# Building one-hot sets in two rings, with two weighted copies on POOL and the first normalisation inside the build

## The chip, the cores and the metric

The kernel runs as one program on one core of a Trainium2 chip. The metric is the device time of one execution in microseconds (us); lower is better. The core has five engines with instruction streams of their own: TensorE (PE), VectorE (DVE), ScalarE (ACT), GpSimd (POOL) and SyncE (SP), which here only issues DMAs. They meet through semaphores.

## The reference

Four graph layers run one after the other on 3125 nodes with 256 features, over 50000 edges sorted by their destination. Cut to what matters:

```python
h = relu(layernorm(x))                      # "the first normalisation"
x = x + sage(sage(h).relu())                # mean over incoming edges, twice
h = relu(layernorm(x))
x = x + segment_sum((h @ W)[src] * edge_weight[:, None], dst) + b
h = relu(layernorm(x))
x = x + interaction_layer(h, edge_attr, src, dst)   # sums over edges, layer norm, three-layer MLP
h = relu(layernorm(x))
x = x + h @ W_self + mean_over_edges(top32(h @ W_neigh)[src], dst)
```

Every layer needs sums over edges. The kernel gets them as products with two dense matrices of 3125 x 3125 (padded to 3200 x 3200): entry (s, d) of the count matrix is the number of edges from s to d, that of the weight matrix the sum of their weights.

## The kernel before

**The build.** The first third of the program makes the two matrices. There are 25 chunks (`NT`) of 128 destinations, and each has 8 tiles (`PER`) of 16 destinations (`G`), 200 tiles in all. The edges lie in edge tiles of 128, one edge per partition. For a tile the program walks over the edge tiles that touch it, three at a time (`RING = 3`; I call these three a group, and one edge tile of it a set). For one set, DVE writes two one-hot matrices: S (L877, 128 x 128: which of 128 residues the source has) and Q (L879, 128 x 400: destination and upper part of the source). The edge weight is split into three bf16 parts, W0, W1 and W2, so that their sum is exact; S times each part gives three weighted copies. Before, ACT makes the first two (L622, two instructions per set) and POOL the third (L579, one per set, after a small copy of the three weights, L576). PE then does four products per set: S with Q into the count bank, and the three copies with Q into the weight bank (L1271; its waits are, in this order, for Q, for ACT, for POOL). Where a tile is done, PE raises `s_built` with a tiny product (L1283), ACT copies the counts out of PSUM (`take`, L616) and DVE the weights (L871), both one tile late: the take of tile t-1 stands behind the work for tile t. After eight tiles SP stores the two blocks of the chunk to DRAM (L434, L438). The two PSUM banks of each matrix alternate from tile to tile.

**The ring.** There is one ring of three sets. DVE may write set u of a group when PE has used set u of the group before (`s_used`, wait in L875).

**The walk.** Each engine reads the bounds of its eight loops from a table at the start of a chunk (L350, eight values into registers) and steps through them on its own. PE and POOL loop over chunks; ACT and DVE have a loop whose body holds two chunks.

**Between build and first layer.** After the last tile DVE computes a scale for the first layer from the weights (L954 to L974, with two steps on PE, L1404 and L1408), waits for the last stores (the staging areas lie where the layer writes), and does the first normalisation for all 25 row blocks: statistics (L1000), one square root on ACT (L673), subtract and multiply (L1011), relu and scale (L1016). ACT makes the first f16 part (L679), POOL the second (L591). SP loads the late weights and then the first two count blocks, transposed (L495). Then PE starts the sums of the first layer (L1321), and within tile 1 the first transposes of its result (L1378).

## Time and profile before

| | |
|---|---|
| median of 3 runs | 1917.61 us (1917.14 to 1918.48) |
| the profiled execution | 1919.31 us |
| its span | 1917.4 us |
| PE busy | 1701.7 us, 89% |
| DVE busy | 1092.2 us, 57% |
| ACT busy | 759.1 us, 40% |
| POOL busy | 369.2 us, 19% |

The page of the profile cuts the span in 40 slices of 48 us:

```profile
PE   2999899999990999999997999999989898986996
DVE  5888788888888122222333666666536666665111
ACT  0988888989882111111111222222224333331000
POOL 1555555555553000000000000000011111110000
PEclk8999999999995999999998999999999999997998
```

A digit is the busy share of a slice in tenths, 9 for 90% or more; PEclk is TensorE's granted clock. Slices 2 to 12 are the build. There ACT and DVE stand at eight or nine tenths and POOL at five. In slice 13 PE has a zero: that is the stretch between build and first layer. All the rest of the program keeps PE at nine tenths nearly throughout.

### The profile page before, as it was taken

Reading aid. Unit: us, or ns where it says so; the run is one execution under the profiler, and the core shown is the slowest. Engines: PE = TensorE matmul, PEld = TensorE weight load, DVE = VectorE, ACT = ScalarE, POOL = GpSimd, SP = SyncE. Lnnn points to the kernel's source line nnn. Section 1 sums busy time; section 2 is a strip of 40 time slices with the busy share of each in tenths; the row PEclk is TensorE's granted clock in tenths of the full one; section 3 lists DMA queues with packets and bytes.
Section 4 is the critical chain, followed back from the end, with each engine's and each line's share of the span. In section 5 each row is a group of like instructions: output and inputs, shape, how many; then the busy total and the mean of one; then the engine's idle time right before and its main releaser. Section 6 shows DMA issues by size and latency. Waiting matters only on the chain.

```text
span 1917.4 us, 47392 instructions
## 1 busy us (share of the span) xinstructions
PE 1701.7 (89%) x11659; PEld 1292.2 (67%) x11660; DVE 1092.2 (57%) x3183; ACT 759.1 (40%) x2194; POOL 369.2 (19%) x982
## 2 busy tenths in 40 slices
PE   2999899999990999999997999999989898986996
PEld 1555555555550777777886888888867676764885
DVE  5888788888888122222333666666536666665111
ACT  0988888989882111111111222222224333331000
POOL 1555555555553000000000000000011111110000
PEclk8999999999995999999998999999999999997998
DMA  2544455445445556553334556565421212110444
GB/s 57 151 147 140 126 155 158 125 125 151 147 146 151 138 171 171 171 171 103 120 132 138 145 153 187 151 179 164 138 90 54 71 54 71 55 68 16 143 150 153
DMA packets 302401, 246.05 MB, mean 128 GB/s; under 512 B 144042, under 2 KB 286182, under 8 KB 302310
## 3 DMA queue, kind: packets, MB, share of 16 engines
q1 hardware_dynamic: 302310, 245.19, 43.0%
q14 instruction: 77, 0.63, 0.1%
q8 instruction: 14, 0.23, 0.0%
HBM read 138.17 MB, written 99.31 MB: 124 GB/s over the span
## 4 chain that ended last, share of the span: by engine, by line
issue 61%; PE 25%; DVE 5%; ACT 2%; POOL 2%; DVEq 1%; ACTq 1%; DMA 1%; SPq 0%; POOLq 0%
PE ps L1271 17%; PE ps L1321 7%; POOL work L601 2%; ACT front L622 2%; DVE front L879 1%; ACT work L616 1%; DVE front L877 1%; DMA wgt_blocks<-arena 0%; DVE work L1000 0%; PE ps L1256 0%; DVE arena L1011 0%; ACTq L350 0%; ACTq L359 0%; ACTq L622 0%; DVE arena L808 0%
## 5 line engine op out<-in xcount | busy, mean ns | idle before, releaser
L1321 PE MATMUL ps<-arena 128*128 128x256 f16 (+1 forms) x5000 | 607.1, 275 | 49.8 <-POOL arena L591 40.2
L1321 PEld LDWEIGHTS ps<-arena 128*128 128x128 f16 x5000 | 489.7, 98 | 147.2 <-issue 77.5
L1271 PE MATMUL ps<-front 128*128 128x400 bf16 x2580 | 482.9, 341 | 23.7 <-ACT front L622 20.0
L622 ACT ACTIVATE front<-front 128x128 bf16<-128x128 bf16 x1290 | 408.9, 391 | 57.6 <-issue 32.6
L1271 PEld LDWEIGHTS ps<-front 128*128 128x128 bf16 x2580 | 241.8, 99 | 196.2 <-ACT front L622 32.0
L1315 PE MATMUL ps<-arena 128*128 128x256 f32 x1250 | 281.3, 382 | 0.0
L579 POOL TENSOR_SCALAR front<-front,w_col 128x128 bf16<-128x128 bf16 x645 | 248.8, 392 | 163.0 <-DVE front L877 156.5
L601 POOL TENSOR_TENSOR work<-work 128x256 f32<-128x256 f32 x75 | 55.2, 736 | 1062.0 <-ACT work L742 1062.0
L1315 PEld LDWEIGHTS ps<-arena 128*128 128x128 f32 x1250 | 237.6, 192 | 31.8
L879 DVE TENSOR_SCALAR front<-iota,off_g,front 128x400 bf16<-128x400 f16 x645 | 253.5, 393 | 0.0
L877 DVE TENSOR_SCALAR front<-iota,front 128x128 bf16<-128x128 f16 x645 | 164.6, 255 | 91.0 <-PE ps L1271 70.0
L1456 PE MATMUL ps<-work,front 128*128 128x128 f32 x600 | 87.5, 292 | 38.7 <-POOL work L601 38.6
L871 DVE COPY arena<-ps 128x400 f32<-128x400 f32 x200 | 114.3, 572 | 1.0 <-PE ps L1283 1.0
L1456 PEld LDWEIGHTS ps<-work,front 128*128 128x128 f32 x600 | 77.9, 202 | 48.5 <-POOL work L601 45.9
L1025 DVE TENSOR_SCALAR rdeg<-ps 128x1 f32 (+1 forms) x25 | 4.0, 158 | 179.2 <-PE ps L1321 179.2
L646 ACT ACTIVATE work<-ps 128x256 f32<-128x256 f32 x75 | 28.8, 384 | 189.4 <-PE ps L1293 189.4
L616 ACT ACTIVATE work<-ps 128x400 f16<-128x400 f32 x200 | 96.8, 484 | 0.7 <-PE ps L1283 0.6
L641 ACT ACTIVATE small<-small 128x1 f32<-128x1 f32 x50 | 14.8, 295 | 186.3 <-DVE small L897 186.3
L1213 DVE SCALAR_TENSOR_TENSOR work<-ps,rdeg,arena 128x256 f32<-128x256 f32 x25 | 12.1, 484 | 112.9 <-PE ps L1321 112.9
L742 ACT ACTIVATE work<-ps,mlp_col 128x128 f32<-128x128 f32 x150 | 46.5, 361 | 66.2 <-PE ps L1456 66.1
L1051 DVE SCALAR_TENSOR_TENSOR work<-ps,rdeg_conv,arena 128x256 f32<-128x256 f32 x25 | 12.1, 484 | 93.8 <-PE ps L1321 93.8
L1097 DVE TENSOR_TENSOR e_hot<-iota,e_key 128x2304 bf16<-128x2304 f16 x25 | 64.0, 2559 | 1.9
(189 smaller groups left out, 1571.8 us busy)
## 6 DMA issues: line engine op xcount, KB each, us to landing
arena<-turned_blocks SPq DMA_DIRECT2D x75, 800.0 KB, 4.3
wgt_blocks<-arena SPq DMA_DIRECT2D x25, 1600.0 KB, 8.5
arena<-wgt_blocks SPq DMA_DIRECT2D x25, 1600.0 KB, 8.3
cnt_blocks<-work SPq DMA_DIRECT2D x25, 800.0 KB, 4.2
turned_blocks<-arena SPq DMA_DIRECT2D x25, 800.0 KB, 3.5
e_raw<-edge_features_padded SPq DMA_DIRECT2D x25, 576.0 KB, 7.9
edge_features_padded<-in_edge_attr SPq DMA_DIRECT2D x24, 512.0 KB, 9.6
out<-arena SPq DMA_DIRECT2D x24, 128.0 KB
```

Of the source, the lines that this page charges most:

```text
L579: pool.tensor_scalar(part_of(u, O_SW + 2 * P, P), part_of(u, O_S, P), w_col[:, u:u + 1], 1.0, ALU.mult, ALU.mult).then_inc(s_hotP, 1)
L601: pool.tensor_tensor(GT[l + 1], GT[l], YT, ALU.add).then_inc(s_g, 1)
L616: act.activation(stage_c[par][:, t, :], cnt_ps[t % 2][:, 0:GW], ACT.Copy).then_inc(s_taken, 1)
L622: m = act.activation(part_of(u, O_SW + a * P, P), part_of(u, O_S, P), ACT.Copy, scale=one(col[:, c, :], t))
L871: dve.tensor_copy(stage_w[par][:, t, :], wgt_ps[t % 2][:, 0:GW]).then_inc(s_takenW, 1)
L877: dve.tensor_scalar(part_of(u, O_S, P), iota1[:, 0:P], one(col[:, C_S, :], t), None, ALU.is_equal).then_inc(s_hotS, 1)
L879: dve.tensor_scalar(part_of(u, O_Q, GW), iota1[:, :], one(off_g, n), one(col[:, C_Q, :], t), ALU.add, ALU.is_equal).then_inc(s_hotQ, 1)
L1097: dve.tensor_tensor(e_hot[:, :, :], iota1[:, 0:P].rearrange("p (o d) -> p o d", o=1).broadcast_to([P, EC, P]), e_key[:, :].rearrange("p (t ...
L1271: return pe.matmul(out_, left, right, start=False, stop=True, skip_group_check=True)
L1315: m = pe.matmul(agg[par][:, 0:D], BLK32[par][:, b * P:(b + 1) * P], ZFULL[0][:, b * D:(b + 1) * D], start=(b == 0), stop=(b == NT - 1), sk ...
L1321: m = pe.matmul(agg[par][:, 0:wide], BLK16[par][:, b * P:(b + 1) * P], ZH[zin(i)][:, b * ZW + part * D:b * ZW + part * D + wide], start=(b ...
L1456: m = pe.matmul(mlp_ps[:, o * P:(o + 1) * P], W[:, k, o * P:(o + 1) * P], GT[l][:, k * P:(k + 1) * P], start=(k == 0), stop=(k == 1))
```

## The change

- There are two rings of three sets, and tile i of a chunk uses ring i % 2. The second lies in `e_part`, a tile that the third layer uses later. DVE keeps for each ring the number of sets after which it is free, and waits for that.
- POOL makes the copies for W1 and W2. It waits for all three S of a group and then issues two products of 128 x 3 x 128 elements, S by the weight broadcast along each set. The small copy of the weights and the drain before it go. PE waits for them apart, for W1 and for W2.
- ACT makes only the W0 copy, one instruction per set, and takes both matrices out of PSUM.
- The first normalisation of block c-1 is spread over chunk c on DVE, in five steps behind tiles 1, 2, 4, 5 and 6. The third step waits for a square root that ACT does behind tile 4. ACT makes the first part of block c-2 behind tile 2, POOL the second part behind tile 4. The multiplication by `H_SCALE` is folded into the square root.
- SP issues the two transposing loads of the first count blocks before the store of the last chunk.
- The scale of the first layer is computed at the start of that layer, on DVE in front of its first row step and on PE behind the sums of tile 0.

```diff
-        ring = front[:, 6 * NCOL:6 * NCOL + RING * SETW // 2].bitcast(BF16)
+        ring0 = front[:, 6 * NCOL:6 * NCOL + RING * SETW // 2].bitcast(BF16)
...
+        ring1 = e_part[:, :, :, :].rearrange("p t a f -> p (t a f)")[:, 0:RING * SETW]
+        ring = [r.rearrange("p (u s) -> p u s", u=RING) for r in (ring0, ring1)]
...
@@ SP
+            for n in range(2):
+                sp.wait_ge(s_store_c[n], 16)
+                sp.dma_start_transpose(BLK16[n].rearrange("p (b d) -> p b d", d=P),
+                                       cnt_dram[n * P:(n + 1) * P, :]).then_inc(s_blk[n], 16)
             store(NT - 1, 0)
...
@@ POOL
-                def weigh_last(k, u, t, i):
-                    if u == 0:
-                        pool.drain()
-                        chain(pool.tensor_copy(w_col[:, :], col[:, C_W2, bass.ds(t, RING)]))
-                    wait(pool, s_hotS, k + (u + 1))
-                    pool.tensor_scalar(part_of(u, O_SW + 2 * P, P), part_of(u, O_S, P), w_col[:, u:u + 1], 1.0,
-                                       ALU.mult, ALU.mult).then_inc(s_hotP, 1)
+                def weigh_sets(k, u, t, i):
+                    if u:
+                        return
+                    wait(pool, s_hotS, k + RING)
+                    plain = ring[i % 2][:, :, O_S:O_S + P]
+                    for a, col_of in ((1, C_W1), (2, C_W2)):
+                        into = ring[i % 2][:, :, O_SW + a * P:O_SW + (a + 1) * P]
+                        by = col[:, col_of, bass.ds(t, RING)].rearrange("p (t o) -> p t o", o=1)
+                        pool.tensor_tensor(into, plain, by.broadcast_to([P, RING, P]), ALU.mult
+                                           ).then_inc(s_hotP[a - 1], RING)
+                def after(t):
+                    if not isinstance(c, int) and t == 4:
+                        second(c - 2)
...
@@ ACT
             def take(c, par, t):
                 wait(act, s_built, c * PER + (t + 1))
                 act.activation(stage_c[par][:, t, :], cnt_ps[t % 2][:, 0:GW], ACT.Copy).then_inc(s_taken, 1)
+                act.activation(stage_w[par][:, t, :], wgt_ps[t % 2][:, 0:GW], ACT.Copy).then_inc(s_takenW, 1)
             def weigh(k, u, t, i):
                 wait(act, s_hotS, k + (u + 1))
-                for a, c in enumerate((C_W0, C_W1)):
-                    m = act.activation(part_of(u, O_SW + a * P, P), part_of(u, O_S, P), ACT.Copy,
-                                       scale=one(col[:, c, :], t))
-                m.then_inc(s_hotA, 1)
+                act.activation(part_of(i, u, O_SW, P), part_of(i, u, O_S, P), ACT.Copy, scale=one(col[:, C_W0, :], t)
+                               ).then_inc(s_hotA, 1)
+            def first_deviation(n):
+                wait(act, s_var0, n + 1)
+                act.activation(sd, mv[:, 1:2], ACT.Sqrt, bias=eps_first, scale=1.0 / H_SCALE ** 2).then_inc(s_std0, 1)
...
+                def after(t):
+                    late(t)
+                    if not (isinstance(c, int) and c == 0) and t == 4:
+                        first_deviation(c - 1)
+                    if not (isinstance(c, int) and c < 2) and t == 2:
+                        first_high(c - 2)
...
@@ DVE
+            def first_norm(n, step):
+                if step == 0:
+                    dve.bn_stats(bn, node(X, n))
+                elif step == 1:
+                    dve.drain()
+                    dve.bn_aggr(mv, bn).then_inc(s_var0, 1)
+                elif step == 2:
+                    wait(dve, s_std0, n + 1)
+                    dve.reciprocal(rs, sd)
+                elif step == 3:
+                    dve.drain()
+                    dve.tensor_scalar(node(R_, n), node(X, n), mv[:, 0:1], rs, ALU.subtract, ALU.mult)
+                else:
+                    dve.drain()
+                    dve.tensor_scalar(node(R_, n), node(R_, n), 0.0, None, ALU.max).then_inc(s_zD, 1)
+            norm_at = {1: 0, 2: 1, 4: 2, 5: 3, 6: 4}
...
                 def hot(k, u, t, i):
-                    wait(dve, s_used, k + (u + 1))
+                    was = dve.snap(free_at[i % 2], min_val=0, max_val=1 << 20)
+                    wait(dve, s_used, was + (u + 1))
...
             def sage1(n, g, par, half, at0, at1, at2):
+                if isinstance(n, int) and n == 0:
+                    convolution_scale()
```

The program order of three engines shows where the work stands now. A row is one instruction: its line, its operation, what it writes and reads, and the semaphores it waits for; rows named ISA or REGISTER_ALU only reckon with registers.

DVE, before, from the last Q of one tile to the first S of the next (`front` holds the ring, `arena` the staging area):

```order
L879 TENSOR_SCALAR front<-iota,off_g,front 128x400
L363 ISA
L359 REGISTER_ALU
L359 COMPARE_AND_BRANCH
L247 REGISTER_ALU
L871 COPY arena<-ps 128x400 [waits tile_built]
L359 ISA
L359 UNCONDITIONAL_BRANCH
L359 ISA
L877 ISA [waits onehots_used]
L877 TENSOR_SCALAR front<-iota,front 128x128
```

DVE, of the change, the same place between tile 4 and tile 5 of a chunk (`e_part` is the second ring):

```order
L924 TENSOR_SCALAR front<-iota,off_g,front 128x400
L927 ISA
L360 REGISTER_ALU
L360 COMPARE_AND_BRANCH
L904 RECIPROCAL small<-small 128x1 [waits first_deviation_ready]
L360 ISA
L360 UNCONDITIONAL_BRANCH
L919 ISA
L922 ISA [waits onehots_used]
L922 TENSOR_SCALAR e_part<-iota,front 128x128
```

The take has left DVE; behind tile 4 stands the reciprocal, which waits for ACT, in front of all three sets of tile 5.

ACT, of the change, the last W0 copy of tile 4 in chunk 1 and what follows it:

```order
L634 ACTIVATE front<-front 128x128
L364 ISA
L360 REGISTER_ALU
L360 COMPARE_AND_BRANCH
L628 ACTIVATE work<-ps 128x400 [waits tile_built]
L629 ACTIVATE arena<-ps 128x400
L639 ACT_TABLE_LOAD
L639 ACTIVATE small<-small 128x1 [waits first_variance_ready]
```

The square root stands behind both takes of tile 3, and the first of these waits until PE has finished tile 3. The table load stands in chunk 1 only.

POOL, before, one group:

```order
L576 ISA
L576 COPY w_col<-front 128x3
L247 REGISTER_ALU
L579 TENSOR_SCALAR front<-front,w_col 128x128 [waits s_ready]
L247 REGISTER_ALU
L579 TENSOR_SCALAR front<-front,w_col 128x128 [waits s_ready]
L247 REGISTER_ALU
L579 TENSOR_SCALAR front<-front,w_col 128x128 [waits s_ready]
```

POOL, of the change, one group:

```order
L594 ISA [waits s_ready]
L594 TENSOR_TENSOR front<-front 128x3x128
L594 ISA
L594 TENSOR_TENSOR front<-front 128x3x128
L364 ISA
L360 REGISTER_ALU
L360 COMPARE_AND_BRANCH
```

Three short instructions with a wait for each set have become two long ones behind a single wait for all three sets.

## Rows read from the trace of the kernel before

**Rows 1.** Stretches: us, busy of each engine, granted clock, DMA share, GB/s

```profile
46.00:578.00 532.00, 488.42 (x3178) 283.00 (x3178) 442.12 (x1487) 473.94 (x1490) 293.37 (x859) 0.97 0.48 143
115.00:118.00 3.00, 3.00 (x14) 1.43 (x13) 1.12 (x4) 2.40 (x8) 0.75 (x2) 0.52 0.25 84
281.00:284.00 3.00, 3.00 (x21) 1.77 (x20) 2.11 (x7) 3.00 (x11) 1.12 (x3) 1.00 0.18 59
1450.00:1454.00 4.00, 2.44 (x18) 1.96 (x17) 3.61 (x14) 1.71 (x6) 1.14 (x2) 1.00 0.00 0
```

**Rows 2.** The page's costliest groups: count, busy us, mean ns, idle before

```profile
L1271 PE MATMUL ps<-front 128*128 128x400 bf16 x2580 | 482.9, 341 | 23.7 <-ACT front L622 20.0
...
L641 ACT ACTIVATE small<-small 128x1 f32<-128x1 f32 x50 | 14.8, 295 | 186.3 <-DVE small L897 186.3
```

**Rows 3.** Timeline of the build, two ordinary tiles: start, us, instruction

```profile
300.81 0.26 DVE L877 TENSOR_SCALAR front<-iota,front 128x128 bf16<-128x128 f16 x1
...
301.26 2.19 PE L1271 MATMUL ps<-front 128*128 128x400 bf16 x12
301.27 0.38 POOL L579 TENSOR_SCALAR front<-front,w_col 128x128 bf16<-128x128 bf16 x1 [0.29 <-DVE front L877]
...
302.47 0.25 DVE L877 TENSOR_SCALAR front<-iota,front 128x128 bf16<-128x128 f16 x1
...
302.93 0.25 DVE L877 TENSOR_SCALAR front<-iota,front 128x128 bf16<-128x128 f16 x1
...
303.45 2.20 PE L1271 MATMUL ps<-front 128*128 128x400 bf16 x12
303.60 0.26 DVE L877 TENSOR_SCALAR front<-iota,front 128x128 bf16<-128x128 f16 x1
...
304.62 0.48 ACT L616 ACTIVATE work<-ps 128x400 f16<-128x400 f32 x1
...
305.00 1.27 ACT L622 ACTIVATE front<-front 128x128 bf16<-128x128 bf16 x4
```

**Rows 4.** Timeline, a tile of two groups and the chunk boundary behind it

```profile
107.14 4.23 PE L1271 MATMUL ps<-front 128*128 128x400 bf16 x24
...
112.33 0.19 PE L1256 MATMUL ps<-zeros 128*128 128x1 bf16 x2 [0.96 <-issue]
...
113.88 1.86 ACT L622 ACTIVATE front<-front 128x128 bf16<-128x128 bf16 x6 [2.92 <-issue]
...
114.62 3.38 PE L1271 MATMUL ps<-front 128*128 128x400 bf16 x11 [1.68 <-ACT front L622]
```

**Rows 5.** POOL's groups by shape, whole span

```profile
L579 POOL TENSOR_SCALAR front<-front,w_col 128x128 bf16<-128x128 bf16 x645 | 248.8, 392 | 163.0 <-DVE front L877 156.5 <-issue 3.7
L601 POOL TENSOR_TENSOR work<-work 128x256 f32<-128x256 f32 x75 | 55.2, 736 | 1062.0 <-ACT work L742 1062.0
L576 POOL COPY w_col<-front 128x3 f32 x215 | 44.9, 209 | 76.4 <-issue 76.4
L591 POOL TENSOR_TENSOR arena<-arena x25 | 16.3, 683 | 31.0 <-ACT arena L679 31.0
```

**Rows 6.** Timeline from the end of the build into the first layer

```profile
578.67 1.21 DVE L954 TENSOR_REDUCE scale<-W_early 128x2 f32<-128x1024 f32 x1
...
588.01 0.17 DVE L974 TENSOR_SCALAR scale<-scale 128x2 int32<-128x2 int32 x1
...
588.56 8.27 DVE L1000 BATCH_NORM_STATS2 work<-arena 128x6 f32<-128x256 f32 x25 [0.38 <-DMA wgt_blocks<-arena]
...
601.25 1.95 DVE L1011 TENSOR_SCALAR arena<-arena,work  x5 [0.54 <-issue]
...
604.30 3.14 DVE L1011 TENSOR_SCALAR arena<-arena,work  x5
...
625.83 9.90 PE L1321 MATMUL ps<-arena 128*128 128x257 f16 x68 [40.17 <-POOL arena L591]
...
635.57 0.60 PE L1378 MATMUL ps<-ident,work 128*128 128x128 f32 x4
```

More of the change, by code:

```diff
@@ L371, in after @@
                     take(c, par, t - 1)
-                elif not isinstance(c, int):
+                elif not (isinstance(c, int) and c == 0):
                     take(c - 1, 1 - par, PER - 1)
@@ L632, in _ @@
             chunk(0, 0, 0)
-            with act.Fori(0, NPAIR) as j:
+            chunk(1, 0, 1)
+            chunk(2, 1, 0)
+            with act.Fori(1, NPAIR) as j:
                 chunk(j * 2 + 1, j, 1)
@@ L878, in hot @@
                                       ALU.is_equal).then_inc(s_hotS, 1)
-                    dve.tensor_scalar(part_of(u, O_Q, GW), iota1[:, :], one(off_g, n), one(col[:, C_Q, :], t),
+                    dve.tensor_scalar(part_of(i, u, O_Q, GW), iota1[:, :], one(off_g, n), one(col[:, C_Q, :], t),
                                       ALU.add, ALU.is_equal).then_inc(s_hotQ, 1)
-                wait(dve, s_store_w[par], half * 16)
-                walk(dve, mybir.EngineType.DVE, c, hot, after=one_tile_late(take, c, par))
@@ L885, in _, with after @@
-            hot_and_take(0, 0, 0)
-            with dve.Fori(0, NPAIR) as j:
-                hot_and_take(j * 2 + 1, j, 1)
-                hot_and_take(j * 2 + 2, j + 1, 0)
-            take(NT - 1, 0, PER - 1)
+                    if u == RING - 1:
+                        dve.reg_add(free_at[i % 2], step_of[mybir.EngineType.DVE], RING)
+                def after(t):
+                    if not isinstance(c, int) and t in norm_at:
+                        first_norm(c - 1, norm_at[t])
+                walk(dve, mybir.EngineType.DVE, c, hot, after=after)
@@ L892, in _ @@
+            hot_sets(0)
+            for j in range(NT // SB):
+                dve.wait_ge(s_x[j], 16 * (1 + (j == NT // SB - 1)))
+            with dve.Fori(1, NT) as c:
+                hot_sets(c)
+            for k in range(5):
+                first_norm(NT - 1, k)
             chain = drained(dve)
-            dve.sem_inc(s_zD, CR)
             dve.sem_inc(s_aggfree, CR)
```

134 lines of the change are left out of this document (59 added, 75 removed).

## The prediction

> **What bounds the kernel now.** I read the granted clock and the busy time by stage first, then the costliest groups, then the timeline of two ordinary tiles, of a chunk boundary and of the stretch behind the build. The build lasts 532 us, 46 to 578, with PE busy for 488 of them and ACT for 474 [rows 1]. PE is its bound: a group of 12 products takes 2.19 us, and the next group follows with no gap [rows 3]. 2580 products are 215 groups [rows 2] in 200 tiles, so 15 groups are the second one of their tile. 200 groups at 2.19 and 15 at about 2.07 (a tile of two takes 4.23 less the tail of its last product [rows 4]) give 469 us. The other 63 us lie at the boundaries of the chunks. At every one PE reads its table, 0.96 us [rows 4], 24 us in all. At every second one ACT stands for 2.92 us with no releaser that the profile shows, PE then waits 1.68 us for it [rows 4]; over the build PE waits 20 us for ACT [rows 2]. And behind most of these waits PE runs at half speed: the stretch behind the one shown was granted 0.52, where another kept 1.00 [rows 1]. Of eleven such boundaries eight show the fall, each about 3.3 us long; the two rows are one of each kind. The start takes the rest.
>
> Behind the build PE has nearly nothing to do for 47.7 us, until the last second part of the normalised rows lets it go at 625.83 [rows 6].
>
> **What goes behind the build.** The normalisation leaves this stretch, but two things stay in DVE's way. It must still wait for the store of the last weight block, which released it at 588.56 [rows 6]. Only then does it do the scale, now behind that wait and not beside it. The scale took from 578.67 to 588.18, 9.5 us [rows 6]. So it ends at about 588.6 + 9.5 = 598.1. The row step of tile 0 takes about 1.1 us more, and PE's first transposes come at about 599.2. Before they came at 635.57 [rows 6]. PE's own path is shorter: takes, square root, three DVE steps, ACT's and POOL's part of block 24 are some 4 us behind the build, tile 0 then takes 7.3 us (50 of the 68 products that took 9.90 [rows 6]), and it waits for the scale at about 589. The saving is 635.6 - 599.2 = 36.4 us, less 0.4 for the last take, which ACT does second: **-36 us**. The store sets it, not the normalisation.
>
> **What POOL's product costs.** No row has this shape. A two-input product of 256 f32 elements took 736 ns, one with an f16 operand 683, a copy of three elements 209 [rows 5]. Taking 209 as fixed, that is 2.06 and 1.85 ns per element, and for 384 elements 1.00 and 0.92 us. I take X = 0.95 us. Bounds: three times the slope of the one-input instruction, 0.209 + 3 x 0.183 = 0.76, and three whole ones, 3 x 0.392 = 1.18 [rows 5].
>
> The Trainium skill, "GPSIMD Engine Reference", section 3.1, has about 2.6 cycles per element for a two-input operation, because both inputs come through one read port, and elementwise work as Vector's job. An estimate from that figure and its 1.2 GHz is 0.83 us plus a fixed part, some 1.04 us with the row's 209 ns. The trace's 2.06 ns per element agrees with it; the sum below would be 39 x 2 x 0.09 = 7 us higher.
>
> **What an ordinary tile does.** Let 0 be the start of PE's group. It has used its third set at 2.19. DVE writes the third S of the group after next 0.15 later (303.60 against 303.45), for 0.26; POOL starts 0.20 behind the end of an S (301.27 against 300.81 + 0.26) [rows 3]. So POOL starts at 2.80 and its second product is there at 2.80 + 2 x 0.95 + 0.08 = 4.78. With two rings it is for the group that starts at 4.38, whose fourth product, the first that needs it, is due at 4.38 + 0.51 = 4.89. The tile passes, with 0.1 us to spare. POOL is busy 1.9 of 2.19 us. ACT has two takes at 0.38 apart (304.62, 305.00) and three copies at 0.31, 1.7 us. DVE has three pairs at 0.46 (302.47, 302.93) [rows 3]. Steady tiles cost nothing new, but nothing has room.
>
> **Second groups of a tile.** Both groups of such a tile lie in the same ring, so the reserve of the second ring is not there. The second group is due at 2.07, its fourth product at 2.58, and POOL is ready at 4.78: 2.2 us of waiting. Before, POOL and ACT followed set by set, and this tile showed no gap [rows 4]. 15 x 2.2 = **+33 us**.
>
> **The reciprocal behind tile 4.** Let 0 now be the end of tile 3 on PE, where tile 4 starts. ACT can take then: two takes, and the square root starts at 0.06 + 2 x 0.38 = 0.82 and ends, with 295 ns [rows 2], at 1.12. DVE, which had finished tile 4's sets about 1.7 us before, does the reciprocal at 1.16 to 1.32. Only then may it write tile 5's sets, though their ring has been free since 0. Third S: 1.32 + 2 x 0.46 + 0.26 = 2.50; POOL 2.70, ready at 2.70 + 1.90 + 0.08 = 4.68. PE has done tile 4 at 2.19 and needs it at 2.70: 2.0 us. Tile 6 recovers, since PE is now late and its ring long free. Queued behind the waiting reciprocal are all sets of tile 5, and for them wait ACT, POOL and PE. 24 chunks x 2.0 = **+48 us**.
>
> **Chunk boundaries.** PE's 0.96 us stays. ACT's stop of 2.92 us begins now behind two takes, at 0.06 + 0.86, and the first W0 copy, one instead of two, ends near 4.2; PE needs it at 2.19 + 0.96 and some 0.4 for the opening of the tile and the first product, 3.6. The wait falls from 1.68 to about 0.7: 11 x 1.0 = **-11 us**. With 1.7 us of idle time rather than 2.6 I let the eight falls of the clock go: 8 x 1.65 = **-13 us**. Bound: none of this, 0.
>
> **The clock behind new waits.** There are 39 new waits of about 2 us. Behind single gaps of 1.5 us, as in 1450 to 1454, the clock stays 1.00; behind 2.6 us of them within 3.3 it fell in eight of eleven cases [rows 1]. I take a quarter of 39, at 1.65 us (3.3 us at half): **+16 us**. Bounds 0 and 64.
>
> **Small items.** The first group needs all three S and both products, the table load for the square root comes once into ACT's stream: **+2 us**. ACT's first part, POOL's second part (0.7 us, behind tile 4, where POOL waits anyway), DVE's other four norm steps and the two early loads lie beside PE's work: 0 each. If that cover were gone, the norm steps would be 1.6 us per chunk.
>
> **Sum.** 33 + 48 - 11 - 13 + 16 + 2 = +75 in the build, -36 behind it: +39. The profiled execution took 1919.3 (span 1917.4 and 1.9 around it), 1.7 above the median of the runs, 1917.6. The forecast is 1919.3 + 39 = **1958 us**.
>
> **Rivals.**
> 1. *Cheap products on POOL: faster.* Place: the same 39 waits. If 16-bit operands halve the two-input rate, X is about 0.5, the waits fall by 0.9 us to 1.3 and 1.1: 20 + 26 us, no fall of the clock. 46 - 24 + 2 - 36 = -12: 1907. It decides from X = 0.66, where the sum without falls of the clock is zero (81 - 78 x 0.29 - 24 + 2 - 36). For it: f16 made L591 7% cheaper than L601 [rows 5]. Against: that is far from half. Chance 0.13; with half of it, within 0.2%, 0.05.
> 2. *Dear products: POOL becomes the bound.* At X = 1.18 the tile is 0.36 us late per two groups, and POOL needs 2.36 us per group: 0.18 x 176 = 32 us more, and 39 x 0.46 = 18 on the waits: 2008; half-way 1980. For it: the broadcast and the three-part pattern are in no row. Chance 0.17.
> 3. *POOL slows DVE.* Five L1011 took 1.95 us with POOL idle and 3.14 us beside its two-input products [rows 6]. If S and Q suffer as much, a pair takes 0.74 us, a group 2.2, and DVE has no room for the norm steps: 1.5 us x 24 = 36, 1994. Against: an S takes 0.25 or 0.26 us whether POOL works or not, though on one input only [rows 3]. Chance 0.15. The Trainium skill, "GPSIMD Engine Reference", table of section 1, says that the SBUF interfaces are shared with Vector, to the harm of Vector instructions in a 2-port mode or with two inputs; L1011's slowing agrees, whether S and Q run so no row shows.
>
> **Chances and range.** Forecast with its own range 1935 to 1978: 0.50. With the rivals: faster by over 0.2% 0.13, within 0.2% (3.8 us, about what a measurement can tell) 0.05, slower 0.82. The bounds reach from about 1910 to over 2000; 1914 to 1996 leaves out two in ten.
>
> **What would show it.** In the changed profile: PE waits of about 2 us for POOL's product, once per chunk in tile 5 and in the second groups, and a DVE wait of near 3 us for ACT at the reciprocal (if these are under 1 us, the forecast is wrong); POOL's product at 0.9 to 1.0 us; a build of some 607 us; PE's start about 4 us behind the build, a stop of 4 us for the scale behind tile 0, and the first transposes 21 us behind the build's end. If ordinary tiles take more than 2.25 us, rival 2 or 3 holds: the length of S and Q tells which.

## The result and the profile after

The changed kernel takes 1982.72 us (median of 4 runs, 1979.91 to 1984.05), the kernel before 1917.38 beside it: a ratio of 1.034, 95% interval 1.0323 to 1.0358. It is slower by 65 us, where 39 were forecast (1958, range 1914 to 1996). The profiled execution took 1981.51 us, with a span of 1979.6.

The costliest groups of the page of the changed kernel, in the columns of [rows 2]:

```profile
L1300 PE MATMUL ps<-e_part 128*128 128x400 bf16 x1332 | 270.6, 335 | 81.1 <-POOL e_part L594 80.0
L1300 PE MATMUL ps<-front 128*128 128x400 bf16 x1248 | 246.7, 335 | 38.7 <-POOL front L594 34.2
L594 POOL TENSOR_TENSOR e_part<-e_part,front 128x384 bf16<-128x384 bf16 x222 | 181.5, 838 | 148.4 <-DVE e_part L922 147.0
L924 DVE TENSOR_SCALAR front<-iota,off_g,front 128x400 bf16<-128x400 f16 x312 | 157.8, 506 | 0.0
L924 DVE TENSOR_SCALAR e_part<-iota,off_g,front 128x400 bf16<-128x400 f16 x333 | 155.4, 467 | 0.0
L922 DVE TENSOR_SCALAR e_part<-iota,front 128x128 bf16<-128x128 f16 x333 | 114.4, 344 | 40.5 <-PE ps L1300 23.4
L922 DVE TENSOR_SCALAR front<-iota,front 128x128 bf16<-128x128 f16 x312 | 118.3, 379 | 26.6 <-issue 15.7
```

One by one, PE's 2580 products take what they took (335 ns in the mean, before 341). But before them PE now stands idle for 120 us, 114 of them until POOL is done, where it was 24 [rows 2]. And the 645 S and 645 Q, whose work is unchanged, add up to 545.9 us on DVE (the last four rows), where the page of the kernel before has 418.1:

```profile
L879 DVE TENSOR_SCALAR front<-iota,off_g,front 128x400 bf16<-128x400 f16 x645 | 253.5, 393 | 0.0
L877 DVE TENSOR_SCALAR front<-iota,front 128x128 bf16<-128x128 f16 x645 | 164.6, 255 | 91.0 <-PE ps L1271 70.0
```

(These sums are larger than DVE's busy time in the build, because the record of an S or Q begins before that of the one in front has ended.) POOL in its turn waits for DVE. So the two engines hold each other up, and PE waits behind both.

The build as one stretch of the changed kernel, in the columns of [rows 1]:

```profile
46.00:678.00 632.00, 506.88 (x3177) 265.69 (x3178) 508.43 (x1412) 426.81 (x1092) 365.80 (x453) 0.99 0.42 122
```

It ends 100 us later than in [rows 1], with 66 us more of DVE's time (although DVE no longer takes the weights) and at a granted clock of 0.99 rather than 0.97. The clock is not the reason. Exactly, from PE's first opening of an accumulator to its last `s_built`, the build went from 533.3 to 632.9 us, +99.6. The stretch between its end and the first transposes got shorter, -36.8 (below). The two make 62.8 us; the span grew by 62.2.

Where the 100 us lie shows a table of the times between two openings of PE's accumulators, summed over the tiles of a kind:

| kind of tile | count | before, us (mean) | after, us (mean) | difference |
|---|---|---|---|---|
| chunk 0 | 8 | 26.1 | 28.6 | +2.5 |
| two groups of sets | 14 | 65.7 (4.69) | 97.1 (6.94) | +31.4 |
| tile 0 of a chunk | 23 | 82.1 (3.57) | 54.5 (2.37) | -27.6 |
| tile 5, behind the reciprocal | 22 | 48.7 (2.21) | 87.5 (3.98) | +38.8 |
| tile 7, with the boundary | 21 | 65.6 (3.12) | 66.7 (3.18) | +1.1 |
| all others | 112 | 245.1 (2.19) | 298.5 (2.67) | +53.4 |

The largest term is the last row, tiles in which nothing special happens. (Tile 6, behind the first row step of the normalisation, is among them with 2.85 us in the mean; the other 89 take 2.62, before 2.19.) The timeline of one, after (start, us, instruction, idle before it and its releaser), beside [rows 3]:

```profile
625.38 1.61 POOL L594 TENSOR_TENSOR e_part<-e_part,front 128x384 bf16<-128x384 bf16 x2 [1.22 <-DVE e_part L922]
...
625.88 0.38 DVE L922 TENSOR_SCALAR front<-iota,front 128x128 bf16<-128x128 f16 x1 [0.46 <-issue]
...
626.18 0.93 DVE L924 TENSOR_SCALAR front<-iota,off_g,front 128x400 bf16<-128x400 f16 x1
...
627.03 0.24 DVE L922 TENSOR_SCALAR front<-iota,front 128x128 bf16<-128x128 f16 x1
...
627.19 0.37 DVE L924 TENSOR_SCALAR front<-iota,off_g,front 128x400 bf16<-128x400 f16 x1
...
627.49 0.24 DVE L922 TENSOR_SCALAR front<-iota,front 128x128 bf16<-128x128 f16 x1
...
627.94 0.92 DVE L922 TENSOR_SCALAR e_part<-iota,front 128x128 bf16<-128x128 f16 x1
627.99 1.67 POOL L594 TENSOR_TENSOR front<-front 128x384 bf16<-128x384 bf16 x2 [1.00 <-DVE front L922]
```

Read POOL and DVE together. POOL's two products run from 625.38 to 626.99. In this time DVE, which needs 0.37 us for a Q, gets one S and one Q done, and the Q takes 0.93 and ends just behind POOL's second product. From 627.03 on DVE runs at its usual pace again, and reaches the third S of the next group at 627.49. That lets POOL go at 627.99, and the S that begins beside it takes 0.92 rather than 0.24. One group lasts 627.99 - 625.38 = 2.61 us: 1.61 of products, and 1.00 in which POOL waits for DVE to catch up. PE needs 2.19 [rows 3].

The durations of all S on one ring, of all products on it (ns, least, median and most):

```profile
L922 DVE TENSOR_SCALAR e_part<-iota,front x333: 240/248/923, 47.9 to 674.4; 128x128 bf16<-128x128 f16 x167
...
L594 POOL TENSOR_TENSOR e_part<-e_part,front x222: 825/826/888, 50.3 to 675.7; 128x384 bf16<-128x384 bf16 x111
```

The median of S hides it, the most of 923 (before: 400) and the mean of 344 and 379 show it. POOL's product is shorter than the 0.95 us that were taken.

Tile 5 of a chunk and the reciprocal in front of it, after:

```profile
616.62 0.50 ACT L628 ACTIVATE work<-ps 128x400 f16<-128x400 f32 x1 [0.55 <-PE ps L1310]
...
617.40 0.30 ACT L639 ACTIVATE small<-small 128x1 f32<-128x1 f32 x1
...
617.73 0.16 DVE L904 RECIPROCAL small<-small 128x1 f32<-128x1 f32 x1 [1.90 <-ACT small L639]
...
619.62 1.66 POOL L594 TENSOR_TENSOR e_part<-e_part,front 128x384 bf16<-128x384 bf16 x2 [1.59 <-DVE e_part L922]
...
620.50 0.34 PE L1300 MATMUL ps<-e_part 128*128 128x400 bf16 x1 [0.94 <-POOL e_part L594]
```

It is the chain of the prediction, link by link: take, square root, reciprocal, sets, products, PE. And the end of the build, the counterpart of [rows 6]:

```profile
678.13 0.17 PE L1310 MATMUL ps<-zeros 128*128 128x1 bf16 x1
...
682.54 7.31 PE L1348 MATMUL ps<-arena 128*128 128x257 f16 x50 [4.25 <-POOL arena L581]
...
688.48 1.22 DVE L1002 TENSOR_REDUCE scale<-W_early 128x2 f32<-128x1024 f32 x1 [7.70 <-DMA wgt_blocks<-arena]
...
698.95 1.11 PE L1405 MATMUL ps<-ident,work 128*128 128x128 f32 x4
```

PE starts 4 us behind the build, waits behind tile 0 for the scale, which waits for the store, and the first transposes come 20.7 us behind the end of the build, where they came 57.5 us behind it.

### The profile page after: what moved, and what is told of

Read it like the earlier page. It is cut to its first block, busy times and chain, and to the rows that moved or that the text cites. A ratio compares the mean times of both kernels' runs of the same rounds, so it can differ in the third digit from the quotient of the medians.

```text
span 1979.6 us, 44443 instructions
## 1 busy us (share of the span) xinstructions
PE 1722.1 (87%) x11659; PEld 1275.7 (64%) x11660; DVE 1126.9 (57%) x3007; ACT 702.5 (35%) x1773; POOL 425.7 (22%) x553
## 4 chain that ended last, share of the span: by engine, by line
issue 62%; PE 16%; DVE 7%; POOL 7%; DVEq 4%; POOLq 3%; SPq 0%; ACT 0%; DMA 0%; ACTq 0%
PE ps L1300 8%; PE ps L1348 7%; POOL e_part L594 2%; POOL front L594 2%; POOL work L612 2%; DVE e_part L922 2%; DVE e_part L924 1%; DVE front L924 1%; DVE front L922 1%; POOLq L360 1%; POOLq L351 1%; DVEq L360 1%; DVEq L900 1%; DVEq L924 1%; POOLq L594 1%
## 5 line engine op out<-in xcount | busy, mean ns | idle before, releaser
L1300 PE MATMUL ps<-e_part 128*128 128x400 bf16 x1332 | 270.6, 335 | 81.1 <-POOL e_part L594 80.0
L1300 PE MATMUL ps<-front 128*128 128x400 bf16 x1248 | 246.7, 335 | 38.7 <-POOL front L594 34.2
L1300 PEld LDWEIGHTS ps<-e_part 128*128 128x128 bf16 x1332 | 120.9, 97 | 193.0 <-POOL e_part L594 135.7
L594 POOL TENSOR_TENSOR e_part<-e_part,front 128x384 bf16<-128x384 bf16 x222 | 181.5, 838 | 148.4 <-DVE e_part L922 147.0
L1300 PEld LDWEIGHTS ps<-front 128*128 128x128 bf16 x1248 | 112.8, 97 | 136.4 <-POOL front L594 73.8
L594 POOL TENSOR_TENSOR front<-front 128x384 bf16<-128x384 bf16 x208 | 170.3, 839 | 117.9 <-DVE front L922 117.9
L924 DVE TENSOR_SCALAR e_part<-iota,off_g,front 128x400 bf16<-128x400 f16 x333 | 155.4, 467 | 0.0
L634 ACT ACTIVATE e_part<-e_part,front 128x128 bf16<-128x128 bf16 x333 | 128.0, 400 | 72.5 <-DVE e_part L922 63.7
L634 ACT ACTIVATE front<-front 128x128 bf16<-128x128 bf16 x312 | 121.2, 400 | 51.0 <-DVE front L922 40.7
L922 DVE TENSOR_SCALAR e_part<-iota,front 128x128 bf16<-128x128 f16 x333 | 114.4, 344 | 40.5 <-PE ps L1300 23.4
L922 DVE TENSOR_SCALAR front<-iota,front 128x128 bf16<-128x128 f16 x312 | 118.3, 379 | 26.6 <-issue 15.7
L629 ACT ACTIVATE arena<-ps 128x400 f32<-128x400 f32 x200 | 99.6, 498 | 0.0
```

Source lines behind the costliest of these rows:

```text
L594: pool.tensor_tensor(into, plain, by.broadcast_to([P, RING, P]), ALU.mult).then_inc(s_hotP[a - 1], RING)
L629: act.activation(stage_w[par][:, t, :], wgt_ps[t % 2][:, 0:GW], ACT.Copy).then_inc(s_takenW, 1)
L634: act.activation(part_of(i, u, O_SW, P), part_of(i, u, O_S, P), ACT.Copy, scale=one(col[:, C_W0, :], t)).then_inc(s_hotA, 1)
L922: dve.tensor_scalar(part_of(i, u, O_S, P), iota1[:, 0:P], one(col[:, C_S, :], t), None, ALU.is_equal).then_inc(s_hotS, 1)
L924: dve.tensor_scalar(part_of(i, u, O_Q, GW), iota1[:, :], one(off_g, n), one(col[:, C_Q, :], t), ALU.add, ALU.is_equal).then_inc(s_hotQ, 1)
L1300: return pe.matmul(out_, left, right, start=False, stop=True, skip_group_check=True)
```

## The experiments

All ratios are against the kernel before, run beside each kernel (medians of 1916.2 to 1918.2). The theory under test: a two-input product on POOL shuts DVE's S and Q out while it runs. The rivals: POOL's chain alone is too long (rival 2 in a milder form), or the rings or the places of the normalisation cost the time.

**m_ports: DVE's instructions alone and beside POOL.** A measurement kernel that computes nothing of the reference. One stream on DVE, alone, beside eight products of POOL and beside sixteen of its one-input instructions. Its core:

```python
dve.tensor_scalar(hot[:, h, 0:P], iota16[:, 0:P], key[:, q:q + 1], None, ALU.is_equal)        # S, 24 times
pool.tensor_tensor(weighted[:, j, :, :], plain, by.broadcast_to([P, 3, P]), ALU.mult)         # 8 times
pool.tensor_scalar(weighted1[:, j, :], plain[:, 0, :], weight[:, 0:1], 1.0, ALU.mult, ALU.mult)  # 16 times
```

> Measures one thing by itself and computes nothing of the reference: DVE runs streams of one instruction, alone and beside eight two-input products of POOL (128 x 3 x 128) or sixteen one-input ones (128 x 128). Theory A (a two-input product of POOL and a DVE instruction of this kind shut each other out): 24 S take about 4 us alone and beside the one-input work, but beside the products each product lets one or two DVE instructions through, so that S and Q streams last until the products end, near 6.6 us for eight at 0.82. Rival B (POOL's products only lengthen the chain from S to PE): S beside the products takes 4 us like S alone. Open: which DVE instructions are shut out; an instruction that reads PSUM, or one with two inputs, may not be.

The groups of the three stretches (S alone, beside products, beside one-input instructions), as on the page:

```profile
L51 DVE TENSOR_SCALAR hot<-iota,key 128x128 bf16<-128x128 f16 x24 | 4.0, 247 | 1.3 <-POOLq L82 1.3
...
L51 DVE TENSOR_SCALAR hot<-iota,key 128x128 bf16<-128x128 f16 x9 | 6.5, 796 | 0.1
L92 POOL TENSOR_TENSOR weighted<-plain,weight 128x384 bf16<-128x384 bf16 x8 | 6.3, 825 | 4.2 <-DVE hot L51 4.2
...
L95 POOL TENSOR_SCALAR weighted<-plain,weight 128x128 bf16<-128x128 bf16 x16 | 5.7, 376 | 2.8 <-DVE hot L51 2.8
L51 DVE TENSOR_SCALAR hot<-iota,key 128x128 bf16<-128x128 f16 x24 | 4.4, 264 | 0.1
```

In 6.5 us beside eight products DVE gets 9 S done, where alone it does 24 in 4.0. The 796 ns are a mean: eight S of 862 to 884 ns (865 in the mean), one per product, and a ninth of 243 that begins when POOL is done. POOL loses nothing by it (6.31 us for eight, as it takes alone). Beside one-input instructions S takes 264 ns in the mean, every second one 285. Other streams, one per product again: Q goes from 381 to 889 ns, an f32 `tensor_scalar` of 256 from 410 to 918, a two-input f32 `tensor_tensor` from 424 to 1043. Of these the last lengthens POOL's eight products too, to 7.87 us, the f32 `tensor_scalar` to 6.65 and Q to 6.44. A copy out of PSUM (12 in 5.87 us) and the statistics (12 in 4.02) did not slow at all. It is not a mean slowing of some per cent, but one DVE instruction let through per product.

The two forms of POOL differ in length too, 384 elements against 128. A shorter two-input instruction, of 256 elements, stands in the build of k6_dve_w1 (below), among POOL's one-input ones:

```profile
144.07 0.69 POOL L583 TENSOR_TENSOR arena<-arena  x1 [0.20 <-issue]
144.15 0.66 DVE L923 TENSOR_SCALAR e_part<-iota,front 128x128 bf16<-128x128 f16 x1
```

The S that begins beside it takes 0.66 us, about as long as the POOL instruction, and so do 18 others in that run (624 to 664 ns); beside one-input instructions of the same run the median is 243. A one-input instruction of 384 elements was not run, so that its length alone would do no harm is not shown.

**e_recip: the reciprocal two tiles later.** What share has its place? The reciprocal goes behind tile 5, the deviation one tile earlier in ACT's stream, so that it is ready in time:

```diff
-                    if not (isinstance(c, int) and c == 0) and t == 4:
+                    if not (isinstance(c, int) and c == 0) and t == 3:
...
-            norm_at = {1: 0, 2: 1, 4: 2, 5: 3, 6: 4}
+            norm_at = {1: 0, 2: 1, 5: 2, 6: 3, 7: 4}
```

> The changed kernel with the square root behind tile 3 and the reciprocal and the two row steps of the normalisation behind tiles 5, 6 and 7. Theory A: the wait of DVE for ACT goes, tile 5 falls from 3.88 us to the 2.6 to 2.9 of its neighbours, 24 x 1.2 = 29 us less, about 1954 us; ordinary tiles stay at 2.61. Rival (the row step itself, slowed by POOL, costs the time wherever it stands): no more than 10 us less.

1966.56 us, ratio 1.0248 (1.022 to 1.0277): 16 us gained, where 29 were expected. Tile 5 fell from 3.98 to 3.01 us (22 of them: -21), but tile 0 rose from 2.37 to 2.76 (+9), since the row steps now run there. Its build as one stretch:

```profile
46.00:663.00 617.00, 506.20 (x3176) 265.10 (x3177) 539.66 (x1412) 424.07 (x1092) 367.22 (x453) 1.00 0.43 125
```

DVE is busy for 31 us more than in the changed kernel, with the same 1412 instructions, and the rise lies in S and Q (580 us by the sum of their four rows, against 546). I read it so that DVE's work, moved out of a wait, meets more of POOL's products; that was not tested by itself.

**e_one: one product of POOL's two.** e_recip, without the product for W1; PE uses the W2 copy in its place. So the W1 part is missing from the weight matrix, and the W2 part is in it twice; all other work is the same.

```diff
-                    for a, col_of in ((1, C_W1), (2, C_W2)):
+                    for a, col_of in ((2, C_W2),):
...
-                    for a, s in enumerate((s_hotA, *s_hotP)):
+                    for a, s in enumerate((s_hotA, s_hotP[1], s_hotP[1])):
```

> As e_recip, and POOL's product for W1 is left out; PE multiplies with the W2 copy in its place, so the W1 part of the weights is missing from the result. Theory A: DVE is shut out for 0.8 us per group instead of 1.65, ordinary tiles fall from 2.61 to PE's own 2.19 and second groups wait 0.8 less: 170 x 0.42 + 15 x 0.8 = 83 us below e_recip, about 1870. Rival B (only the chain S, two products, PE): by the chain two products need 2.26 us per tile, so it takes at most 170 x 0.07 + 12 = 24 us off, about 1930, unless something else slows DVE.

1863.76 us, ratio 0.9721 (0.9692 to 0.975), 103 below e_recip. Ordinary tiles take 2.10 us, PE's own rate, and the build as one stretch is

```profile
46.00:555.00 509.00, 472.90 (x3177) 261.39 (x3178) 434.43 (x1412) 400.81 (x1092) 193.81 (x238) 0.99 0.52 152
```

with DVE busy for 105 us less, though none of its instructions was touched. The second product cost DVE that time. This fits the theory (1870); a chain on POOL alone should have given 1930. It is 54 us faster than the kernel before, but the making of the W1 copies is left out, so this only bounds what the rest of the change can be worth.

**k2_rings: two rings in the kernel before, nothing else.** Are the rings themselves dear?

```diff
+        ring1 = e_part[:, :, :, :].rearrange("p t a f -> p (t a f)")[:, 0:RING * SETW]
...
-            return ring[:, u * SETW + at:u * SETW + at + width]
+            return ring[i % 2][:, u, at:at + width]
```

> The kernel before with the two rings alone: ACT makes two copies, POOL one with its one-input instruction, DVE takes the weights, normalisation behind the build. Theory A: rings cost nothing by themselves; DVE's lead of one more group covers part of the stop of ACT at every second chunk: 0 to 25 us less than before, 1895 to 1917. Rival C (the rings and their registers slow DVE, and are the cause of the slower tiles): ordinary tiles go up from 2.17 towards 2.6, 1950 or more.

1911.29 us, ratio 0.9969 (0.9951 to 0.9987): 0.3% faster, so the rings are not the cause. Its waits between 80 and 540 us (waited for, total us, times, longest):

```profile
DVE front L884 <- issue: 40.6, 11, 3.9
...
PE ps L1280 <- DVE front L886: 23.6, 11, 2.5
```

The tiles ran at 2.10 us, and the boundaries took it back. ACT's stop [rows 4], which PE waited for, is gone from PE's waits, and at every second boundary stands one of DVE, up to 3.9 us long.

**e_psum: DVE takes its row of steps from PSUM.** If S and Q with a PSUM source are not shut out, as the copy in m_ports was not, e_recip should lose its ordinary-tile cost.

```diff
+            steps_ps = ps[:, 6, 0:GW]
+            dve.tensor_copy(steps_ps, iota1[:, :])
...
-                    dve.tensor_scalar(part_of(i, u, O_S, P), iota1[:, 0:P], one(col[:, C_S, :], t), None,
+                    dve.tensor_scalar(part_of(i, u, O_S, P), steps_ps[:, 0:P], one(col[:, C_S, :], t), None,
```

> As e_recip, and DVE reads the row of steps for S and Q from PSUM instead of SBUF (f32 there). By the separate measurement a DVE instruction that reads PSUM is not shut out by POOL's products, but it is slower by itself: Q about 0.5 us instead of 0.3, a pair about 0.7, three pairs 2.1 us per group. Theory A (shutting out makes the ordinary tile 2.61): ordinary tiles fall to 2.2 or 2.3 although every DVE instruction takes longer, 170 x 0.35 = 60 us below e_recip, about 1905. If anything else made the tile, longer DVE instructions can only add: 1967 or more.

A miss: 2024.03 us, ratio 1.0561 (1.0545 to 1.0577). The reason is in its timeline:

```profile
404.13 0.69 DVE L927 TENSOR_SCALAR e_part<-ps,off_g,front 128x400 bf16<-128x400 f32 x1
...
404.47 1.61 POOL L594 TENSOR_TENSOR e_part<-e_part,front 128x384 bf16<-128x384 bf16 x2 [2.88 <-DVE e_part L925]
404.74 0.34 DVE L925 TENSOR_SCALAR front<-ps,front 128x128 bf16<-128x128 f32 x1
404.99 0.69 DVE L927 TENSOR_SCALAR front<-ps,off_g,front 128x400 bf16<-128x400 f32 x1
```

The premise held: beside POOL's products from 404.47 on S and Q take what they take without them, over the whole build 325 to 352 and 676 to 693 ns. But a pair takes 0.86 us, three take 2.58, and DVE became the bound. I had estimated a Q from PSUM at 0.5 us. The experiment shows that the shutting-out can be avoided; what the kernel would take without it, it does not show.

**e_scale: the scale ahead of the wait for the store.** The prediction said that the store sets the first transposes. The scale goes right behind the last row step:

```diff
+            convolution_scale()
...
-                if isinstance(n, int) and n == 0:
-                    convolution_scale()
```

> The changed kernel with the scale of the first layer begun by DVE right behind its last row step, before it waits for the last stores; PE's part stays behind tile 0. The build is untouched. The store then ends beside the scale: DVE is ready for the first row step about 3.4 us sooner (PE's part can only start when tile 0 is done, at 689.9): 1979. If the stores set the start alone it would be 9.5 us: 1973. If the scale was hidden anyway: 1983.

1982.24 us, ratio 1.0344 (1.0328 to 1.036): no change to the kernel after, where 3 us were expected. PE in this kernel:

```profile
695.90 0.66 PE L1404 MATMUL ps<-ident,work 128*128 128x128 f32 x4 [1.83 <-DVE work L1057]
...
704.13 3.58 PE L1347 MATMUL ps<-arena 128*128 128x257 f16 x18 [2.33 <-DMA arena<-cnt_blocks]
707.50 0.87 PE L1404 MATMUL ps<-ident,work 128*128 128x128 f32 x4
```

The first transposes come 3 us earlier (698.95 after). Two rows on PE waits 2.33 us for the load of a count block, and the next transposes stand at 707.50, in the kernel after at 707.29. The store's wait hid a load that was late anyway.

**k4 and k3_one_ring: the old division with the normalisation in the build.** If the products are the cause, then two rings, ACT's two copies, POOL's one-input third, DVE's weight takes and the normalisation at e_recip's places (with the scale as in e_scale) should beat both. k3_one_ring is k4 with the second ring taken away:

```diff
-            return ring[i % 2][:, u, at:at + width]
+            return ring[0][:, u, at:at + width]
```

> Two rings, the old division of the set making (ACT W0 and W1, POOL W2 with its one-input instruction, DVE takes the weights), and from the change the normalisation inside the build (square root behind tile 3, reciprocal and row steps behind tiles 5 to 7), the early loads, and the scale as in e_scale. Theory A: nothing on POOL shuts DVE out, ordinary tiles stay near 2.1 as in k2_rings (1911), and the end gives its 36 + 3 us; ACT, at 2.24 us of work per tile, pays for its 0.7 us per chunk with up to 15 us: 1872 to 1887. If the spread normalisation by itself disturbs the build as it did in the changed kernel (tile 5 at +1.2 us): 1900.

> As k4 with one ring. If the rings are worth what k2_rings showed (6 us), 6 to 10 us above k4, 1880 to 1895. If the second ring is what lets the normalisation fit in, since DVE with one ring has no lead to spend on it, each norm step of 0.4 us goes to PE: 24 x 1.5 = 36 us, 1915.

k4 missed: 1923.83 us, ratio 1.003 (1.0017 to 1.0042). Its build ends at 620, and the end gives its 40 us back. Its waits, 80 to 540 us:

```profile
DVE front L925 <- issue: 40.2, 10, 4.2
...
PE ps L1306 <- DVE front L927: 26.1, 10, 3.0
PEld ps L1306 <- ACT e_part L633: 23.6, 81, 0.7
```

DVE's stop at every second boundary stands as in k2_rings; new are 81 short waits of PE's loads for ACT, which with a take and six copies per tile was already full (busy for 474 of 532 us in [rows 1]) and has no room for its part of the normalisation: tiles 3 and 4 took 2.47 and 2.32 us in the median. The granted clock of its build is 0.95, that of k2_rings 0.97. These account for a part of the miss; the rest stays open. k3_one_ring took 1947.74, ratio 1.0171 (1.0158 to 1.0185). It is 24 us above k4, between the two expected differences (6 to 10, and 36): with the normalisation inside, the second ring does pay.

**k6_dve_w1 and k6b_dve_w1_all: POOL one-input, W1 made by DVE.** From the start S x W1 is one instruction of DVE, a comparison and a factor. k6 is the changed kernel with both ACT takes, POOL's W2 as three one-input instructions, W1 of the first two sets on DVE and of the third on ACT, normalisation and scale as in k4:

```diff
+                    if u < ON_DVE:
+                        dve.tensor_scalar(part_of(i, u, O_SW + P, P), iota1[:, 0:P], one(col[:, C_S, :], t),
+                                          one(col[:, C_W1, :], t), ALU.is_equal, ALU.mult
...
+                    pool.tensor_scalar(part_of(i, u, O_SW + 2 * P, P), part_of(i, u, O_S, P), w_col[:, u:u + 1], 1.0,
+                                       ALU.mult, ALU.mult).then_inc(s_hotP[1], 1)
```

> The changed kernel with no two-input product on POOL in the build: DVE makes the W1 copy of two sets straight from the row of steps (is_equal, then times the weight), ACT that of the third set beside W0 and both takes, POOL makes W2 with its one-input instruction; DVE keeps a loop body of one chunk. Reciprocal late and scale early, as in k4. Theory A: nothing shuts DVE out, its work is 3 x 0.46 + 2 x 0.17 = 1.7 us per tile and 1.6 per chunk, ACT's 1.7 + 0.3 = 2.0 us; ordinary tiles at 2.1 to 2.2, second groups without a wait, chunk boundaries without the 4 us stop of the two-chunk body: build of about 505 to 520 us instead of 532, with the 37 + 3 us at the end 1850 to 1870. If the loss of the changed kernel had another cause than POOL's products (rings, spread normalisation, the takes on ACT), it stays above 1917.

> As k6_dve_w1 with the W1 copy of all three sets on DVE: DVE 1.9 us per tile and 1.6 per chunk, 2.1 in the mean, ACT 1.7. Theory A with DVE as the bound: tiles of 2.1 to 2.3, 0 to 25 us above k6_dve_w1. If DVE's lead of two tiles covers it, the same as k6_dve_w1.

k6_dve_w1 took **1896.93 us**, ratio 0.9886 (0.9869 to 0.9904): it beats both kernels, though by less than expected. Its build, 46 to 590 us, is still 12 us longer than before, and its first transposes come at 606.97. A part of this is ACT: in front of the first W0 copy at every second boundary it stands again for 2.6 to 2.9 us (the profile puts this down to DVE, but in the one before 154.62 the S that ACT needs was done 2 us sooner), PE waits 15.7 us for these copies in 13 times (80 to 540 us), and behind such boundaries the granted clock falls to half again, nine times for 3.4 us, where in the changed kernel's build it falls once. k6b_dve_w1_all, with W1 of all sets on DVE (`ON_DVE = 3`), took 1934.79, ratio 1.009 (1.0073 to 1.0107), 38 us above k6 where 0 to 25 were expected: tiles 1 to 6 take 2.3 to 3.0 us in the median, with DVE as the bound.

**k6_product: k6 with W2 as one two-input product.** Engine, data and all other work are k6's; only the form of POOL's instruction changes (and with it that one waits for three S, and that the copy of the weights goes):

```diff
-                    pool.tensor_scalar(part_of(i, u, O_SW + 2 * P, P), part_of(i, u, O_S, P), w_col[:, u:u + 1], 1.0,
-                                       ALU.mult, ALU.mult).then_inc(s_hotP[1], 1)
+                    pool.tensor_tensor(ring[i % 2][:, :, O_SW + 2 * P:O_SW + 3 * P], ring[i % 2][:, :, O_S:O_S + P],
+                                       by.broadcast_to([P, RING, P]), ALU.mult).then_inc(s_hotP[1], RING)
```

> As k6_dve_w1 (1897), and POOL makes W2 with one two-input product of 128 x 3 x 128 per group instead of three one-input instructions and the copy of the weights. POOL's own work falls from 1.3 + 0.2 to 0.8 us per group. Theory A (only the form of the instruction counts): DVE, at 1.7 us per tile plus 0.2 for its share of the normalisation, is shut out for up to 0.8 more and becomes the bound: ordinary tiles 2.4 to 2.6, 170 x 0.3 = 50 us more, 1930 to 1960. If POOL's load or the wait for three S were what counted, it is the same or faster: 1885 to 1900.

1943.24 us, ratio 1.014 (1.0117 to 1.0162): 46 us above k6. The builds of k6_dve_w1 and, behind it, of k6_product, each as one stretch, in the columns of [rows 1]:

```profile
46.00:590.00 544.00, 495.97 (x3180) 274.75 (x3179) 471.40 (x1842) 445.84 (x1307) 318.03 (x883) 0.97 0.49 143
```

```profile
46.00:641.00 595.00, 497.21 (x3175) 266.44 (x3176) 534.60 (x1842) 461.92 (x1307) 194.15 (x238) 0.99 0.45 131
```

POOL's work falls by 124 us, and DVE's, with the same 1842 instructions, rises by 63. In the timeline of k6_product

```profile
329.71 0.83 POOL L593 TENSOR_TENSOR front<-front 128x384 bf16<-128x384 bf16 x1 [1.67 <-DVE front L923]
...
332.19 0.89 DVE L923 TENSOR_SCALAR front<-iota,front 128x128 bf16<-128x128 f16 x1
332.20 0.83 POOL L593 TENSOR_TENSOR e_part<-e_part,front 128x384 bf16<-128x384 bf16 x1 [1.66 <-DVE e_part L923]
```

the S takes 0.89 us as long as the product lasts, and a group takes 332.20 - 329.71 = 2.49: 0.83 of product and 1.66 of DVE's rest. That is the sum by which the changed kernel's 2.61 came out.

## Why the prediction was right or wrong

**Direction: right, the size partly by luck.** Slower, within the range, with +65 where +39 stood. In the spans it is +62.8, 24 more than forecast, and the largest single term was not among its own: ordinary tiles cost 53 us that the sum had at nothing. They were offset by terms that came out smaller than forecast, above all the clock's 16, of which about 2 came, and the reciprocal's 48, of which 38.8 came.

**Behind the build, -36: right, and by its mechanism.** Measured -36.8, with the store's wait, the scale behind it and the transposes at 20.7 us behind the build against 21. Only e_scale adds that taking the store's wait away gains nothing: a load is late behind it.

**Second groups of a tile, +33: right.** Measured +31.4. It was right partly by luck: with X at 0.83 rather than 0.95 the same sum gives 15 x (2.2 - 0.24) = 29. That DVE's slower sets filled the difference is an argument, not a measurement.

**Reciprocal behind tile 4, +48: too large.** Measured +38.8 in tile 5, of which only 22 x (3.98 - 2.67) = 29 us, or 31 for 24 chunks, stand above what an ordinary tile now takes. The forecast added its wait to a tile of 2.19 us; in tiles that already wait for POOL a part of it is covered. DVE's wait for ACT was forecast near 3 us: this wait, between 80 and 540 us, was 35.7 us in 18 times, 2.0 in the mean and 3.3 at most. e_recip took 21 us from this tile, and got 16 in the end.

**Boundaries -11 and falls of the clock -13: right in size, by luck in the mechanism.** Tile 0 of the chunks gave -27.6. The forecast kept ACT's stop of 2.92 us and let it begin sooner. In the changed kernel the stop is not there at all: apart from one boundary beside a tile of two groups (2.18), ACT's longest idle time at a boundary is 0.84 us. With it went the falls of the clock, which stood at 0.99.

**The clock behind new waits, +16: too large, about 2.** One stretch fell, 89.3 to 92.8, granted 0.51, in the tile 5 of chunk 1, where PE had waited 1.02 us for DVE and 1.14 for POOL. The lower bound of 0 was the right end.

**What an ordinary tile does: the step that failed.** "Steady tiles cost nothing new" stands on two numbers. One, X = 0.95, was on the safe side. The other was DVE's "three pairs at 0.46", taken from [rows 3] where POOL ran one-input instructions. Beside the two-input products a pair takes more than 1 us, and the alternation makes the tile 2.61 to 2.67: +53.4 us, and 10.6 more in the 22 tiles 5. Nothing in the sum stood for that. Some 5 of the 53.4 us lie in tile 6: DVE's other norm steps, which the forecast had at 0, are not quite free either (L907 takes 0.74 us beside POOL).

**Rival 3 had the place, with chance 0.15, and a smaller size.** "A pair takes 0.74 us" took the slowing of L1011 (1.95 to 3.14 us [rows 6]) as a mean factor. With that DVE would need 2.2 us per group and a tile would just pass. The runs show another thing: while a product lasts DVE gets one instruction of this kind through, however short (m_ports: eight S of 862 to 884 ns beside eight products). Two products, 1.61 us in a group of 2.19, then leave DVE about 0.6 us at full pace for the rest of its work, which in the timeline above takes 1.00. The row that spoke against the rival, S unchanged beside POOL, did so "on one input only", and this was the whole point: m_ports has 264 ns beside one form and 865 beside the other.

The Trainium skill, "GPSIMD Engine Reference", table of section 1, names the place: POOL and VectorE share the SBUF interfaces, to the harm of VectorE's 2-port and two-input instructions. The trace agrees for the two-input `tensor_tensor` of m_ports (424 to 1043 ns). S and Q have one input; they suffer too (S from 247 to 865 ns), but whether they run in a 2-port mode no run shows. The table makes no difference by the form of POOL's instruction, and m_ports does. From its section 3.1, 2.6 cycles per element, the prediction had an estimate of 1.04 us for the product; measured are 0.826, so for this product (one operand bf16, the other a broadcast weight) it was too high.

**Rivals 1 and 2.** X came out at 0.83 us, between the forecast and rival 1, which decides at 0.66. POOL was never the bound by its own work: it was busy for 366 of 632 us.

**The signs.** The prediction wrote that ordinary tiles above 2.25 us mean rival 2 or 3, and that the length of S and Q tells which. They were 2.67, and the length told: rival 3's place. A build of 607 us was expected, it was 633.

**Open.** Why ACT or DVE stops for 2.6 to 4.2 us at every second boundary was not tested. The traces have a hint. The page lists a DMA queue that moves instructions (q14). It has 77 packets in the kernel before and 20 in the changed one; k2_rings has 132, k4 131, k6_dve_w1 74. In each of the eleven stops of ACT in the kernel before (80 to 540 us) two such packets begin, of 8 KB, and in each of the eleven of DVE in k2_rings four. So an engine seems to wait there for its own code; ACT and DVE show these stops only where the loop's body holds two chunks, and the changed kernel's DVE has a body of one. Neither that nor why ACT's body of two chunks goes without in the changed kernel was tested. Open too are the rest of k4's miss and of k6's.

## What to carry to other kernels

Before work moves to POOL, look at what DVE executes beside it, and at the form of POOL's instruction: one two-input product kept POOL busy for less time than three one-input instructions and cost the kernel 46 us. "POOL has time left" and "DVE has time left" are not two budgets where one shuts the other out; add them up. A row that shows no harm speaks only for the form of instruction that it shows.

## What the runs showed of the hardware

- POOL's two-input products shut DVE's S and Q out almost whole: eight S of 862 to 884 ns beside eight products, 24 of 247 ns alone. POOL's pace stays the same beside S (6.31 us for eight), and nearly so beside Q (6.44) and an f32 `tensor_scalar` (6.65), but not beside a two-input `tensor_tensor` of DVE (7.87).
- Not touched: DVE's copy out of PSUM (12 in 5.87 us) and its statistics (12 in 4.02 us). Touched little: S beside one-input POOL instructions (264 ns against 247).
- A PSUM source makes Q 0.68 us rather than 0.37, and it stays so beside POOL's products (676 to 693 ns over the build of e_psum).
- POOL multiplies 128 x 384 bf16 by a broadcast f32 weight in 826 ns.
- DVE can stop at a boundary as ACT does in [rows 4]: at every second chunk up to 3.9 us in k2_rings and 4.2 in k4, where its loop's body holds two chunks; 1.5 us at most in the changed kernel, whose body holds one.
